# Recurrent r and c products 32 columns at a time, each half in a PSUM bank of its own

## The reference

```python
x = x + L0(x, cond)                       # shared + routed experts
Z = sigmoid(xz + H @ Whz.T + bhz)
R = sigmoid(xr + H @ Whr.T + bhr)
H_tilda = tanh(xh + R * H @ Whh.T + bhh)
H = Z * H + (1.0 - Z) * H_tilda           # 512 times, one after the other
Y = H @ Whq.T + bhq
x = x + Ys
```

## Time and profile before

| | us |
|---|---|
| median of 3 runs | 1283.78 |
| lowest, highest | 1283.69, 1285.43 |
| span of the profiled execution | 1282.1 |
| VectorE busy in it | 996.5 |
| ScalarE busy in it | 805.1 |
| longest wait in total: t_h (L705) for the c product | 208.2 |

### The profile page before, as it was taken

One profiled execution on the slowest core, in us unless ns is written; L12 is line 12 of the kernel. 1 busy time (PEld: TensorE's weight loads), 2 busy tenths in 40 slices (PEclk: granted clock), 3 DMA queues, 4 the chain that ended last, 5 costly groups with the idle time before them and its releaser, 6 DMA issues.

```text
span 1282.1 us, 84275 instructions
## 1 busy us (share of the span) xinstructions
PE 1255.5 (98%) x35592; PEld 879.3 (69%) x35592; DVE 996.5 (78%) x6111; ACT 805.1 (63%) x4402; POOL 7.4 (1%) x25
## 2 busy tenths in 40 slices
PE   9999999999999999999999999999999999999887
PEld 8876667766667766667767666766666766666554
DVE  6678787787787878778787887777877787877765
ACT  4366666666666666666666666666666666666554
POOL 1000000000000000000000000000000000000000
PEclk9999999999999999999999999999999999999999
DMA  9311011111101111011111101111011111000110
GB/s 272 59 33 44 23 40 27 42 40 34 39 20 42 35 37 45 24 37 27 43 40 34 38 21 43 33 38 45 27 33 27 44 39 33 23 21 26 33 32 11
DMA packets 76185, 51.34 MB, mean 40 GB/s; under 512 B 40608, under 2 KB 73760, under 8 KB 75808
## 3 DMA queue, kind: packets, MB, share of 16 engines
q1 hardware_dynamic: 75128, 45.29, 13.9%
q10 hardware_dynamic: 680, 0.66, 0.2%
HBM read 29.13 MB, written 16.78 MB: 36 GB/s over the span
## 4 chain that ended last, share of the span: by engine, by line
PE 93%; DVE 3%; ACT 2%; issue 1%; DMA 1%; SPq 0%
PE dn_ps L1073 27%; PE up_ps L1100 26%; PE zc_bank L1235 21%; PE r_bank L1235 15%; PE aux L1073 2%; DVE terms L996 2%; PE dn_ps L1107 1%; ACT t_h L705 1%; PE misc L1073 1%; DVE hist L999 1%; DMA x_all<-in_x 1%; ACT t_r L685 0%; DVE t_rT L974 0%; PE zc_bank L1048 0%; DVE rhT L977 0%
## 5 line engine op out<-in xcount | busy, mean ns | idle before, releaser
L974 DVE STREAM_TRANSPOSE t_rT<-t_r 128x32 f32<-128x32 f32 x1024 | 156.1, 191 | 176.6 <-ACT t_r L685 167.4
L685 ACT ACTIVATE t_r<-r_bank 128x32 f32<-128x32 f32 x1024 | 146.3, 195 | 213.9 <-PE r_bank L1235 201.5
L705 ACT ACTIVATE t_h<-zc_bank 128x32 f32<-128x32 f32 x1024 | 146.1, 195 | 208.2 <-PE zc_bank L1235 208.2
L1073 PE MATMUL dn_ps<-we_sb,x_all 128*32 128x256 f32 (+1 forms) x5144 | 274.8, 329 | 0.0
L1235 PEld LDWEIGHTS zc_bank<-whT,rhT 128*8 128x8 f32 x8192 | 118.2, 87 | 177.9 <-DVE rhT L977 176.9
L1235 PE MATMUL r_bank<-whT,hist 128*8 128x64 f32 x8192 | 210.1, 220 | 16.6 <-DVE hist L999 13.6
L1235 PE MATMUL zc_bank<-whT,rhT 128*8 128x64 f32 x8192 | 211.5, 220 | 2.7 <-DVE rhT L977 0.3
L1235 PE MATMUL zc_bank<-whT,hist 128*8 128x64 f32 x8192 | 208.9, 219 | 0.4 <-issue 0.4
L1235 PEld LDWEIGHTS r_bank<-whT,hist 128*8 128x8 f32 x8192 | 117.8, 88 | 111.5 <-DVE hist L999 92.7
L996 DVE STREAM_TRANSPOSE terms<-t_h 128x32 f32<-128x32 f32 x1024 | 156.5, 192 | 39.6 <-ACT t_h L705 20.7
L1073 PEld LDWEIGHTS dn_ps<-we_sb,x_all 128*32 128x32 f32 x5144 | 138.2, 110 | 31.0
(11 more groups left out here) (132 smaller groups left out, 1663.8 us busy)
## 6 DMA issues: line engine op xcount, KB each, us to landing
gate_inputs_by_group<-gru_raw SPq DMA_DIRECT2D x64, 192.0 KB, 2.0
gru_raw<-gate_inputs_by_group SPq DMA_DIRECT2D x256, 48.0 KB
xT_all<-in_x SPq DMA_DIRECT2D x448, 8.0 KB
x_all<-in_x SPq DMA_DIRECT2D x31, 128.0 KB
out<-gru_raw SPq DMA_DIRECT2D x31, 128.0 KB
x_all<-in_L_cond_W1e SPq DMA_DIRECT2D x4, 512.0 KB, 7.5
we_sb<-in_L_cond_W2e SPq DMA_DIRECT2D x4, 512.0 KB, 8.4
xT_all<-in_L_cond_w SPq DMA_DIRECT2D x2, 256.0 KB, 5.6
```

What stands on the lines that cost most here:

```text
L685: act.activation(t_r[:, i, :], r_ps[:, i * Q:(i + 1) * Q], ACT.Tanh, scale=0.5).then_inc(tr_ready, 1)
L705: act.activation(t_h[:, i, :], c_ps[:, i * Q:(i + 1) * Q], ACT.Tanh, scale=-1.0).then_inc(th_ready, 1)
L974: dve.transpose(t_rT[:, i, :], t_r[:, i, :]).then_inc(trT_done, 1)
L1073: done = pe.matmul(ps[Q * j:Q * (j + 1), col:col + cols], lhsT[:, Q * j:Q * (j + 1)], rhs, start=first, stop=last, tile_position=(0, Q * j ...
```

## The change

- The r and c products: each matmul of 64 columns becomes two of 32, `halves_product`. Half i of both gates lies in PSUM bank i (`rc_banks`: r in columns 0 to 31, c in 32 to 63), and r_done and c_done count halves. The order is k = 0: half 0, half 1; k = 1: half 0 (counted), half 1 (counted).
- z has its own bank. The seed of z and c is parted: `seed_c` right behind the two t_r of the same step, `seed_z` (next step's) behind a_row, and `seed_r` (next step's) behind the two t_h. a_row follows t_z directly.
- `misc` is given up: logits, transposes of all x1 tiles and outputs share `aux`, with waits that keep their order. Logits move from r = 15, 19, 21, 23 (one product of 8 instructions each) to 19, 21 and 23 (two at 23). The last output uses dn_ps. For the first pair in the scan r = 15 keeps five ups.

```diff
-        r_bank = ctx.enter_context(nc.psum_tensor("r_bank", [P, 512], F32))
-        zc_bank = ctx.enter_context(nc.psum_tensor("zc_bank", [P, 512], F32))
+        rc_banks = ctx.enter_context(nc.psum_tensor("rc_banks", [P, NI, 512], F32))
+        z_bank = ctx.enter_context(nc.psum_tensor("z_bank", [P, 512], F32))
-        misc = ctx.enter_context(nc.psum_tensor("misc", [P, 512], F32))
-        LOGITS2 = {15: (0, 0), 19: (0, 1), 21: (1, 0), 23: (1, 1)}
+        LOGITS2 = {19: [(0, 0)], 21: [(0, 1)], 23: [(1, 0), (1, 1)]}
@@ SyncE: input rows @@
-                    sp.wait_ge(seeded_zc, TS * n + HALF)
+                    sp.wait_ge(seeded_c, TS * n + HALF)
@@ ScalarE, body @@
                         for i in range(NI):
-                            if i == 0:
-                                act.wait_ge(r_done, TS * n + s + 1)
-                            act.activation(t_r[:, i, :], r_ps[:, i * Q:(i + 1) * Q], ACT.Tanh, scale=0.5).then_inc(tr_ready, 1)
+                            act.wait_ge(r_done, NI * (TS * n + s) + i + 1)
+                            act.activation(t_r[:, i, :], r_both[:, i, :], ACT.Tanh, scale=0.5).then_inc(tr_ready, 1)
+                        seed_c(n, s)
                         act.wait_ge(z_done, TS * n + s + 1)
                         act.activation(t_z[:, :, :].rearrange("p i q -> p (i q)"), z_ps, ACT.Tanh, scale=0.5).then_inc(tz_ready, 1)
+                        act.wait_ge(tz_ready, TS * n + s + 1)
+                        act.activation(a_row[:, :, :], t_z[:, :, :], ACT.Copy, bias=0.5, scale=-0.5).then_inc(a_ready, 1)
                     if after:
...
-                        seed_r(*after)
-                    if scan:
-                        act.wait_ge(tz_ready, TS * n + s + 1)
-                        act.activation(a_row[:, :, :], t_z[:, :, :], ACT.Copy, bias=0.5, scale=-0.5).then_inc(a_ready, 1)
+                        seed_z(*after)
...
                         for i in range(NI):
-                            if i == 0:
-                                act.wait_ge(c_done, TS * n + s + 1)
-                            act.activation(t_h[:, i, :], c_ps[:, i * Q:(i + 1) * Q], ACT.Tanh, scale=-1.0).then_inc(th_ready, 1)
+                            act.wait_ge(c_done, NI * (TS * n + s) + i + 1)
+                            act.activation(t_h[:, i, :], c_both[:, i, :], ACT.Tanh, scale=-1.0).then_inc(th_ready, 1)
...
-                        seed_zc(*after)
+                        seed_r(*after)
@@ TensorE, body @@
-                            done = gate_product(r_ps, 0, hT, k)
-                        done.then_inc(r_done, 1)
-                        pe.wait_ge(seeded_zc, TS * n + s + 1)
+                            if k == 0:
+                                pe.wait_ge(seeded_r, TS * n + s + 1)
+                            halves_product(r_both, 0, hT, k, r_done)
+                        pe.wait_ge(seeded_z, TS * n + s + 1)
...
                             if k == 0:
-                                pe.wait_ge(tz_ready, TS * n + s + 1)
-                            done = gate_product(c_ps, 2, rhT, k)
-                        done.then_inc(c_done, 1)
+                                pe.wait_ge(seeded_c, TS * n + s + 1)
+                            halves_product(c_both, 2, rhT, k, c_done)
+            def halves_product(both, gate, lhsT, k, halves_done):
+
+                for i in range(NI):
+                    done = gate_product(both[:, i, :], gate, lhsT, k, i * Q, (i + 1) * Q)
+                    if k == NI - 1:
+                        done.then_inc(halves_done, 1)
```

More of the change, by code:

```diff
@@ L194, in moe_then_gru @@
         seeded_r = sem("seeded_r")
-        seeded_zc = sem("seeded_zc")
+        seeded_z = sem("seeded_z")
+        seeded_c = sem("seeded_c")
         w13_high_ready = sem("w13_high_ready")
@@ L382, in stages @@
             return 0 <= n < NT, 0 <= n + 1 < NT, 0 <= n - 1 < NT
-        def x1_bank(t):
-            return misc if t % 2 == 0 else aux
         def last_bank(h):
-            return misc if h else aux
+            return dn_ps[h]
         def iterations(body):
@@ L750, in add_base @@
                 dve.wait_ge(logits_done, i + 1)
-                dve.tensor_tensor(logits[:, tiles, :], misc[:, 0:(tiles.stop - tiles.start) * NE].rearrange("p (n e) -> p n e", e=NE),
+                dve.tensor_tensor(logits[:, tiles, :], aux[:, 0:(tiles.stop - tiles.start) * NE].rearrange("p (n e) -> p n e", e=NE),
                                   over_tiles(rbase[:, :], tiles), ALU.add).then_inc(logits_ready, 1)
@@ L1055, in early_logits @@
                 for k in range(KC):
-                    product(misc, NT * NE, NE, condT[:, k, :], rw_sb[:, KC + k, :], k == 0, k == KC - 1)
+                    product(aux, NT * NE, NE, condT[:, k, :], rw_sb[:, KC + k, :], k == 0, k == KC - 1)
                 for i in range(EARLY):
                     for k in range(KC):
-                        last = product(misc, i * NE, NE, xT_all[:, i, k, :], rw_sb[:, k, :], k == 0, k == KC - 1)
+                        last = product(aux, i * NE, NE, xT_all[:, i, k, :], rw_sb[:, k, :], k == 0, k == KC - 1)
                 last.then_inc(logits_done, 1)
@@ L1065, in set_bits @@
                 pe.wait_ge(tr_dve, NTR // 2)
-                for ps in (r_bank, zc_bank):
+                for ps in (rc_banks[:, 0, :], rc_banks[:, 1, :], z_bank):
                     pe.matmul(ps[:, 0:2 * GW], zeros[:, :], zeros[:, 0:2 * GW], start=True, stop=True).then_inc(bits_set, 1)
@@ L1143, in transpose_x1 @@
                 pe.wait_ge(acc_done, turn(t, NGR - 1) + 1)
-                if t < 2:
-                    pe.wait_ge(logits_ready, 1)
-                if t >= EARLY - 2 and t % 2 == 0 and t + 2 < NT:
+                if t % 2 == 0 and t + 2 < NT:
                     pe.wait_ge(logits_ready, t // 2 + 1)
-                if t % 2 == 1 and t > 1:
+                elif t > 2:
                     pe.wait_ge(y_ready, t - 2)
+                else:
+                    pe.wait_ge(x1T_ready[0], 1)
                 for k in range(KC):
-                    done = pe.transpose(x1_bank(t)[:, k * P:(k + 1) * P], x_of(t)[:, k * P:(k + 1) * P], ident[:, :])
+                    done = pe.transpose(aux[:, k * P:(k + 1) * P], x_of(t)[:, k * P:(k + 1) * P], ident[:, :])
                 done.then_inc(x1T_done, 1)
@@ L1172, in tile_logits @@
                     pe.wait_ge(late_xT_ready, t - EARLY + 1)
-                done = product(misc, t % 2 * NE, NE, xT_all[:, place_xT(t), k, :], rw_sb[:, k, :], k == 0, k == KC - 1)
+                    if t % 2 == 0 and t > EARLY:
+                        pe.wait_ge(y_ready, t - 4)
+                    elif t == EARLY:
+                        pe.wait_ge(x1T_ready[1], 1)
+                done = product(aux, t % 2 * NE, NE, xT_all[:, place_xT(t), k, :], rw_sb[:, k, :], k == 0, k == KC - 1)
                 if t % 2 == 1 and k == KC - 1:
@@ L1180, in output @@
                     pe.wait_ge(yst_ready, t + 1)
[L1181 to L1184, removed]
+                    if t + 2 < NT:
+                        pe.wait_ge(x1T_ready[t % 2], t // 2 + 2)
                     else:
@@ L1228, in fill_rest, with gate_product @@
                     keep_busy()
-                if r in LOGITS2 and EARLY <= 2 * p + 2 + LOGITS2[r][0] < NT:
-                    tile_logits(2 * p + 2 + LOGITS2[r][0], LOGITS2[r][1])
-            def gate_product(ps, gate, lhsT, k):
+                for tile, k in LOGITS2.get(r, ()):
+                    if EARLY <= 2 * p + 2 + tile < NT:
+                        tile_logits(2 * p + 2 + tile, k)
+            def gate_product(ps, gate, lhsT, k, begin=0, end=GW):
                 for j in reversed(range(NG)):
-                    done = pe.matmul(ps[Q * j:Q * j + B, :], lhsT[:, k, :], whT[:, gate, k, j * GW:(j + 1) * GW], start=False,
+                    done = pe.matmul(ps[Q * j:Q * j + B, :], lhsT[:, k, :], whT[:, gate, k, j * GW + begin:j * GW + end], start=False,
                                      stop=(k == NI - 1), tile_position=(0, Q * j), skip_group_check=True)
                 return done
+            def halves_product(both, gate, lhsT, k, halves_done):
[3 more added lines that the diff above has]
+                        done.then_inc(halves_done, 1)
             def keep_busy():
```

37 lines of the change are left out of this document (17 added, 20 removed).

## The result

The change made the kernel slower by a third. Its median is 1707.96 us (1701.26 to 1715.86, 4 runs), beside 1283.74 us (1282.86 to 1285.43, 4 runs) for the kernel before: a ratio of 1.3309, with an interval of 1.3268 to 1.3349. The forecast was 1278.5 us, with a range of 1265 to 1293.

What follows compares the result with a forecast made beforehand. Latency was taken to bound both halves of a step, TensorE less than 0.1 us behind. Step terms gave -4.2 us, pairs without routing about -1.2: -5.4 on 1282.1, plus 1.7 carried over, rounded to 1278.5 us; range 1265 to 1293.

Steps and rivals of the forecast that it cites:

- TensorE pays 0.03 more for each of the two products, 0.06 a step: r and c products: eight 32-column rounds of 0.032 us take 0.255 us instead of 0.22.
- whether TensorE keeps up: TensorE's work ahead of c and behind it with five ups: 0.01 us spare each; with six ups TensorE binds.
- all four: The rivals' times, in order: 1270 us (chance 0.25), 1294 (0.2), 1285 (0.15), 1258 (0.05).
- free step: Recurrence steps gaining the full 0.076 us from earlier first-half reads, nine in 32: 2.30 us each.
- three signs of being wrong: z later than 0.27 us after r, t_z still at 0.71, or TensorE waiting on the shared bank.
- Rival 2: r and c products: rounds take 0.036 us or more, TensorE becomes the bound, 1294 us; chance 0.2.
- Rival 1: ScalarE hides the seed of c, a_row comes only 0.02 us late, 1270 us; chance 0.25.
- routing step: Steps with two routing operations on VectorE have no spare, so a_row's 0.06 us delay lengthens them: 2.43 us.
- r = 8: Step whose third up waits for L812, which follows factors: 0.06 us longer.
- The states' copy: L623 between a_row and t_h, once in 16 steps: 0.206 us later, steps near 2.58 us, 6.4 us over 31 steps.
- The sum: Gains and losses over the 32 steps of a tile pair: -261 ns, x 16 pairs = -4.2 us.
- The shared bank and the other small edits: Side products' shared-bank waits cost nothing; tail's banks and third zeroing matmul under 0.1 us once.

Runs made afterwards that it cites:

- change_joint: The whole change, with seed and operand counted in one joint semaphore each for r and c, no second wait: 1580.38 us, 1.2308.
- whole_joint: The changed kernel with r and c again in 64-column matmuls, and one joint semaphore each for r and c: 1295.78 us, 1.0098.
- c_halves_only: The changed kernel with r whole again (64 columns, one bank, one count) and c still in halves: 1484.44 us, 1.1566.
- before_z_in_two: The kernel before with only the z product in two 32-column parts, same bank and count: 1396.39 us, 1.088.

## Why the prediction was wrong

**The step that failed** is "TensorE pays 0.03 more for each of the two products, 0.06 a step". It priced 33,300 more instructions of TensorE (16,386 matmuls, as many weight loads, 526 waits) by their rounds in the array, and at nothing as instructions. The section on whether TensorE keeps up counted array time alone. The row for it stood on the page of before: queue 8 with 281 packets. One packet of 256 instructions lasted before 1282.1 / 281 = 4.56 us; a step used 140 instructions (71,943 over 512 steps), so 256 lasted 4.4 us. The changed step uses 205, and at a step of about 2.39 us 256 of them would have to come every 3.0 us. In no run did fetches come faster than every 3.78 us on the mean; in the changed kernel it was 4.05. No rival named this; all four were arguments about array time and about ScalarE's and VectorE's order.

The Trainium skill, Runtime: NRT & Kernel Launch, Instruction fetch mechanics, says that instructions come in 16 KiB blocks of 256, that the sequencer fetches the next while the current one runs, and that the cost of crossing a boundary is mostly hidden. The trace agrees on the block and on the order of fetches. It disagrees on the cost: hidden in the kernel before (6 stops at 269 marks), 414 us in the changed one. Had the block of 256 been laid beside the 205 instructions a step, there would have been a fifth rival; no row of before has its price.

**The steps that held.** Where no stop disturbs a step, the forecast's own terms are there. ScalarE in a free step of the changed kernel:

```profile
864.55 0.29 ACT L682 ACTIVATE t_r<-rc_banks 128x32 f32<-128x32 f32 x2 [1.72 <-PE rc_banks L1234]
864.74 0.22 ACT L614 ACTIVATE rc_banks<-gru_raw 128x64 f32<-128x64 f32 x1
864.88 0.22 ACT L685 ACTIVATE t_z<-z_bank 128x64 f32<-128x64 f32 x1
865.13 0.26 ACT L687 ACTIVATE a_row<-t_z 128x64 f32<-128x64 f32 x1
...
865.70 0.29 ACT L701 ACTIVATE t_h<-rc_banks 128x32 f32<-128x32 f32 x2 [0.19 <-PE rc_banks L1234]
...
866.87 0.20 ACT L682 ACTIVATE t_r<-rc_banks 128x32 f32<-128x32 f32 x1 [0.46 <-PE rc_banks L1234]
```

None of the forecast's three signs of being wrong appeared: in undisturbed steps z starts 0.24 after r (median; the sign was 0.27), t_z is late as forecast, and no wait of TensorE on the shared bank stands in the recurrence. None of the three looked at the supply of instructions.

- *Products.* A 32-column instruction takes 194 ns on the mean (forecast 0.192). The 32 of c, started at 865.25, last 0.43, so the last starts 0.24 after the first: eight rounds of 0.032 less one, plus the offset of four groups, as taken. t_h starts 0.45 after c (forecast 0.44). Rival 2, rounds of 0.036, is out.
- *ScalarE.* Behind t_r, the seed of c is at 0.19, t_z at 0.33 and a_row at 0.58; the forecast had 0.19, 0.335 and 0.59. Rival 1 is out too.
- *The beat.* From t_r to t_r it is 2.32 here, 2.31 in the mean of undisturbed free steps (forecast 2.30). A routing step has 2.45 (t_r at 834.77 and 837.22; forecast 2.43), r = 8 has 2.47 (forecast 2.465).
- *The states' copy* stands in the way as worked out, t_r to t_r 2.58 (forecast 2.58):

```profile
253.74 0.29 ACT L682 ACTIVATE t_r<-rc_banks 128x32 f32<-128x32 f32 x2 [1.46 <-PE rc_banks L1234]
...
254.63 0.64 ACT L621 ACTIVATE gru_raw<-hist 128x256 f32<-128x256 f32 x1
255.18 0.26 ACT L701 ACTIVATE t_h<-rc_banks 128x32 f32<-128x32 f32 x2
...
256.32 0.29 ACT L682 ACTIVATE t_r<-rc_banks 128x32 f32<-128x32 f32 x2 [0.36 <-PE rc_banks L1234]
```

- *The sum.* Undisturbed, the 32 steps would take some 76.6 us against 76.4 before: +3 us over the kernel, where the forecast had -4.2. So even with an unlimited supply the change would have been about even or a little slower: it moves the read of the first half 0.04 earlier twice a step, and pays it back in the steps in which a_row, the states' copy or a sixth up come last. This is an estimate from about 120 of the 511 steps, few for each place in the cycle and none for one; the same sum in change_joint is 77.1, +11 us. No run had the supply to show it.
- *The shared bank and the other small edits,* costed at nothing, are bounded by whole_joint: with them, the new order and z's bank, but without the split, it is 12 us above before, and its free steps take no longer. The parts were not run one by one.

**What stays open.** Why the fetch of a block is not asked for earlier: it starts 1.15 to 1.95 us (median 1.65) after TensorE enters the block before (median 1.02 in the kernel before), takes about 1.05 us in both kernels, and the block is used 1.25 to 1.5 us after that. These three follow each other and sum to about 4 us; which of them a kernel can shorten, beyond the double wait (1.65 to 1.15 in change_joint), was not tried. Also open is why c_halves_only and before_z_in_two lie 88 us apart with the same number of packets. It is not the steps themselves: undisturbed they sum to 77.2 and 77.1 us per 32. It is the stops, about 200 us in some 270 of them against about 100 us in some 130. c_halves_only's second double wait may make a part, perhaps as much as the 35 us that taking out one gave; nothing shows the rest. And why the floor is 3.8 us in some kernels and 4.1 in others is shown only in so far as the double waits move it (4.05 to 3.78 in the change, 3.92 to 3.83 with z in two).

## What to carry to other kernels

Before a matmul is split, count TensorE's instructions, weight loads and separate waits included, against the time in which they must come: here 256 needed some 3.8 to 4.1 us, 62 to 68 instructions a us. The packets of the instruction queue on the page give the kernel's present rate, and "issue" stops in the middle of a product show that it is spent. A kernel beyond that edge was served by fewer and larger instructions even in work that had slack and got longer by it, and a product that had to wait for two events was better given one semaphore that both count in than a second wait, on TensorE or on the engine before it.

## What the runs showed of the hardware

- TensorE's instructions came in packets of 256. A kernel whose steps used 140 in 2.39 us was not slowed; 8 more a step cost 0.65%, 32 more 8.8% (6.1% without its double wait), 65 more 33%.
- Each call of an fp32 matmul here is two matmuls and two weight loads in that stream: the 16 calls of a split product are 64 instructions.
- The fetch of a packet took about 1.05 us in the kernel before and in the changed one; in the changed kernel the stops ended 1.25 to 1.5 us after a fetch had ended.
- A second semaphore wait ahead of a matmul is an instruction of its own. Taking 1024 of them out of the changed kernel gave 128 us, and the mean fetch went from 4.05 to 3.78 us; taking 512 out of the kernel before gave 2 us.
- A second wait ahead of a VectorE operation on the path cost 0.07 us (0.32 against 0.25).
- Rounds of four column groups with 32 columns started 0.032 us apart, as those with 8 columns did: from 32 columns to 8 nothing was gained.
